# A sparse memory stage: every eighth gathered row is added on VectorE, with split scores, compact keys and a ninth ring place

## The reference

```python
q = (x @ Wq + bq).reshape(-1, 8, 128); q1, q2 = q[..., :64], q[..., 64:]
s1 = einsum('bhc,hnc->bhn', q1, keys[:, 0]); s2 = einsum('bhc,hnc->bhn', q2, keys[:, 1])   # 256 scores each
s1t, i1 = top_k(s1, 8); s2t, i2 = top_k(s2, 8)
scores, best = top_k(s1t[..., :, None] + s2t[..., None, :], 8)    # best 8 of 64 sums
indices = i1 * 256 + i2 at best
inner = einsum('bd,bhkd->bhk', x, w_down[indices])
vals = relu(inner) * softmax(scores)
out = einsum('bhk,bhkd->bd', vals, w_up[indices])
```

## Time and profile before

| what | value |
|---|---|
| median of 3 runs | 3177.79 us (3175.93 to 3196.16) |
| the profiled execution | 3188.18 us, span 3186.4 us |
| busy share of the span: TensorE, VectorE, ScalarE, GpSimd | 83%, 48%, 22%, 32% |
| start of the memory stage (end of the block before) | 2005.4 us |
| first row product of tile 0 | 2134.1 us |
| row products of the stage | 640, in ten tiles |

### The profile page before, as it was taken

How to read it: one execution, slowest core, us unless ns; L and a number is a source line. 1 busy time by engine, 2 the same in 40 slices (tenths; PEclk the granted TensorE clock), 3 DMA queues, 4 the chain that set the end, 5 groups by cost and what they waited for, 6 DMA issues and landing times.

```text
span 3186.4 us, 28032 instructions
## 1 busy us (share of the span) xinstructions
PE 2657.5 (83%) x8756; PEld 1463.4 (46%) x8756; DVE 1516.1 (48%) x3729; ACT 700.5 (22%) x1527; POOL 1010.8 (32%) x823
## 2 busy tenths in 40 slices
PE   2897887998770299999899888789898998998887
PEld 1564555665330044444366455554544544454322
DVE  3556448999200000000122545157657656666675
ACT  0233222121210000110033422123232323322322
POOL 0003343444344200000000000026566556656676
PEclk9898998999895599999999989899999999999999
DMA  9601306676210123023300040038898898889998
GB/s 209 204 0 21 89 1 190 200 216 187 43 7 1 32 78 79 0 62 112 92 1 0 0 148 0 7 110 314 284 329 312 297 314 308 309 311 332 344 366 349
DMA packets 237785, 498.58 MB, mean 156 GB/s; under 512 B 98553, under 2 KB 98928, under 8 KB 233546
## 3 DMA queue, kind: packets, MB, share of 16 engines
q0 software_dynamic: 158720, 336.03, 31.5%
q1 hardware_dynamic: 76425, 156.38, 16.5%
q10 hardware_dynamic: 2550, 5.12, 0.4%
HBM read 476.77 MB, written 20.34 MB: 156 GB/s over the span
## 4 chain that ended last, share of the span: by engine, by line
PE 49%; DMA 26%; DVE 11%; issue 7%; POOL 3%; ACT 2%; another core or an unknown queue 1%; SPq 1%; POOLq 0%; DVEq 0%; ACTq 0%
DMA adj<-e_cnt,e_idx 21%; PE bank L1018 10%; PE bank L1243 10%; PE bank L1233 3%; PE bank L1223 3%; PE bank L1003 2%; PE bank L581 2%; PE bank L1180 2%; PE bank L562 2%; PE bank L550 2%; PE bank L557 2%; PE bank L1192 2%; DVE qv L1471 2%; DMA qv<-in_L_ffn_rows,qv 2%; PE bank L770 1%
## 5 line engine op out<-in xcount | busy, mean ns | idle before, releaser
L283 POOL DMA_INDIRECT adj<-e_cnt,e_idx x160 | 344.2, 2151 | 740.4 <-DMA adj<-e_cnt,e_idx 446.8
L1243 PE MATMUL bank<-qv,stage 125*125 125x512 f32 x640 | 346.2, 633 | 65.6 <-DVE qv L1479 31.2
L1318 ACT ACTIVATE stage<-ident,qv 125x125 f32<-125x125 f32 x640 | 242.4, 397 | 481.7 <-DVE qv L1471 253.6
L1018 PE MATMUL bank<-big,wreg 125*125 125x512 f32 x400 | 173.4, 596 | 159.2 <-DMA wreg<-adj 159.2
L1471 DVE SCALAR_TENSOR_TENSOR qv<-qv 125x512 f32<-125x512 f32 x320 | 237.2, 745 | 143.8 <-DMA qv<-in_L_ffn_rows,biasb 74.4
L1143 POOL MEMSET wreg<- 64x2048 f32 x2 | 3.6, 1800 | 916.2 <-DVE h L700 916.1
L852 DVE SCALAR_TENSOR_TENSOR qv<-wreg,att_b,qv 128x2048 f32<-128x2048 f32 x120 | 276.9, 2349 | 6.9 <-DVE qv L852 0.2
L1149 POOL DMA_INDIRECT qv<-in_L_ffn_rows,qv x160 | 164.8, 1030 | 218.8 <-DVE qv L1413 113.9
L1243 PEld LDWEIGHTS bank<-qv,stage 125*125 125x125 f32 x640 | 113.8, 195 | 208.1 <-ACT stage L1318 91.2
L1149 POOL DMA_INDIRECT qv<-in_L_ffn_rows,biasb x160 | 163.9, 1025 | 112.7 <-PE bank L1243 90.7
L1018 PEld LDWEIGHTS bank<-big,wreg 125*125 125x125 f32 x400 | 75.6, 189 | 257.0 <-issue 257.0
(11 more groups left out here) (220 smaller groups left out, 4232.2 us busy)
## 6 DMA issues: line engine op xcount, KB each, us to landing
wreg<-in_L_gnn_basis SPq DMA_DIRECT2D x60, 1024.0 KB, 5.6
big<-in_L_mix_W SPq DMA_DIRECT2D x4, 4096.0 KB
adj<-wreg SPq DMA_DIRECT2D x5, 2187.5 KB
wreg<-adj SPq DMA_DIRECT2D x10, 1093.8 KB
qv<-adj SPq DMA_DIRECT2D x10, 1093.8 KB
big<-cells_t SPq DMA_DIRECT2D x1, 8750.0 KB
adj<-e_cnt,e_idx POOLq DMA_INDIRECT x160, 3.7
qv<-in_L_ffn_rows,qv POOLq DMA_INDIRECT x160, 5.9
```

What stands on the lines that cost most here:

```text
L283: nc.gpsimd.indirect_dma_start(out=adj, out_offset=bass.IndirectOffsetOnAxis(ap=e_idx[:, g:g + 1], axis=0), in_=e_cnt[:, g:g + 1], in_offs ...
L1018: mm = nc.tensor.matmul(psum[j][0:P, :], slabs[gl][:, j, c, :], zrel[:, c, :], start=(c == 0), stop=(c == COLT - 1))
L1243: nc.tensor.matmul(psum[7][0:P, :], diags[:, s % DRING, :], ring[s % RING][0:P, DIM:ROW], start=(s == 0), stop=(s == SLOTS - 1), skip_grou ...
L1318: nc.scalar.activation(diags[:, s % DRING, :], ident[0:P, 0:P], ACT.Relu, scale=inner[:, s:s + 1]).then_inc(p_diag, 1)
```

## The change

- Every eighth row of a tile (slots 7, 15, ... 63) gets no diagonal and no row product. After its dot VectorE clamps `inner` at zero and adds `inner` times the up half to a running sum `extra` in SBUF (for slot 7 it writes it). `take` adds `extra` to the node's value first, then bank 7. The place is freed by the new semaphore `p_add`.
- The keys are stored compactly (`keys_t`, 8 x 256 columns, both halves on 64 partitions each). A head's score is two matmuls of 64 partitions and 256 columns, into banks 3 and 4, and waits for the search of the head just before. The two memsets go, and four copies of 128 partitions replace eight of 64.
- The space that this frees holds a ninth ring place, used in turn over tile borders.
- TensorE issues a row product one slot later than its place in the order (`LAG`).
- The order moves: transposes at slot 0, queries at slots 1 to 5, scores at 8, 12, ... 36; the search in slots 9 to 39, three steps in four slots, the rest of it from 40 to 48; `take` after dot 1.

```diff
@@ -43,8 +43,7 @@
 SLOTS = PKH * TOPK
-RING = 8
-ROUNDS = SLOTS // RING
+RING = 9
 DRING = 8
...
@@ -155,13 +154,13 @@
-        keybd = wflat[:, 4096:8192].rearrange("p (h n) -> p h n", h=PKH)
+        keys_t = wflat[:, 4096:6144].rearrange("p (h n) -> p h n", h=PKH)
         wqf = wflat[:, 0:4096].rearrange("p (k n) -> p k n", k=KC)
...
         ROW = 2 * DIM
-        ring = [region[0:128, at + ROW * n:at + ROW * n + ROW] for region, at, count in ((qv, 5592, 4), (ctx_flat, 0, 1), (stage, 4048, 1), (big, 18384, 2))
+        ring = [region[0:128, at + ROW * n:at + ROW * n + ROW] for region, at, count in ((qv, 5592, 4), (ctx_flat, 0, 1), (stage, 4048, 1), (big, 18384, 2), (wflat, 6144, 1))
                 for n in range(count)]
...
@@ -1077,26 +1077,49 @@
+        extra = wflat[0:P, 7168:7168 + DIM]
+        BESIDE = 8
...
-        TURN_AT = 1
-        QUERY_AT = [2 + hh for hh in range(PKH)]
-        SCORE_AT = [10 + 3 * hh for hh in range(PKH)]
-        TAIL_AT = 35
-        EXP_AT = 42
+        LAG = 1
+        TURN_AT = 0
+        QUERY_AT = [1 + hh - hh // 2 for hh in range(PKH)]
+        SCORE_AT = [8 + 4 * hh for hh in range(PKH)]
+        SEARCH_AT = SCORE_AT[0] + 1
+        TAIL_AT = SEARCH_AT + 4 * PKH - 1
+        EXP_AT = TAIL_AT + 5
...
-        TAKE_AT = 3
+        TAKE_AT = 1
+        def aside(s):
+            return s % BESIDE == BESIDE - 1
+        def rows_of(pe, n):
+            return n - n // BESIDE if pe else n // BESIDE
+        def freed(engine, n):
+            if aside(n % SLOTS):
+                engine.wait_ge(p_add, rows_of(False, n + 1))
+            else:
+                engine.wait_ge(p_up, rows_of(True, n + 1))
...
-            return 16 * (t * ROUNDS + s // RING + 1)
+            return 16 * ((t * SLOTS + s) // RING + 1)
+        def place(t, s):
+            return (t * SLOTS + s) % RING
...
@@ -1139,16 +1162,14 @@
             pool.wait_ge(m["hat"], ADDS["hat"] + 2 + 2 * TILES)
-            for s in range(2):
-                nc.gpsimd.memset(keybd[64 * s:64 * s + 64, :, NKEYS * (1 - s):NKEYS * (2 - s)], 0.0).then_inc(p_keysS, 1)
             for t in range(TILES):
...
                     if t * SLOTS + s >= RING:
-                        pool.wait_ge(p_up, t * SLOTS + s - RING + 1)
+                        freed(pool, t * SLOTS + s - RING)
                     nc.gpsimd.indirect_dma_start(
-                        out=ring[s % RING], out_offset=None, in_=a["L0_ffn_rows"],
-                        in_offset=bass.IndirectOffsetOnAxis(ap=slots_of[t % 2][:, s:s + 1], axis=0)).then_inc(s_row[s % RING], 16)
+                        out=ring[place(t, s)], out_offset=None, in_=a["L0_ffn_rows"],
+                        in_offset=bass.IndirectOffsetOnAxis(ap=slots_of[t % 2][:, s:s + 1], axis=0)).then_inc(s_row[place(t, s)], 16)
...
@@ -1185,11 +1206,14 @@
                     pe.wait_ge(p_q, t * PKH + hh + 1)
-                    if hh >= 2:
-                        pe.wait_ge(p_top, t * TOPN + 4 * (hh - 1))
+                    if hh:
+                        pe.wait_ge(p_top, t * TOPN + 4 * hh)
                     elif t:
-                        pe.wait_ge(p_top, (t - 1) * TOPN + 4 * (PKH - 1 + hh))
-                    nc.tensor.matmul(psum[3 + hh % 2][0:P, :], pq_t[:, hh, :], keybd[:, hh, :], start=True, stop=True).then_inc(p_s_pe, 1)
+                        pe.wait_ge(p_top, (t - 1) * TOPN + 4 * PKH)
+                    for s in range(2):
+                        rows = slice(64 * s, 64 * s + 64)
+                        mm = nc.tensor.matmul(psum[3 + s][0:P, 0:NKEYS], pq_t[rows, hh, :], keys_t[rows, hh, :], start=True, stop=True)
+                    mm.then_inc(p_s_pe, 1)
                     yield
...
@@ -1239,9 +1263,15 @@
                     pe.wait_ge(p_out, t)
-                pe.wait_ge(p_diag, t * SLOTS + s + 1)
-                nc.tensor.matmul(psum[7][0:P, :], diags[:, s % DRING, :], ring[s % RING][0:P, DIM:ROW], start=(s == 0), stop=(s == SLOTS - 1),
+                if aside(s):
+                    return
+                pe.wait_ge(p_diag, rows_of(True, t * SLOTS + s + 1))
+                nc.tensor.matmul(psum[7][0:P, :], diags[:, s % DRING, :], ring[place(t, s)][0:P, DIM:ROW], start=(s == 0), stop=(s == SLOTS - 2),
                                  skip_group_check=True).then_inc(p_up, 1)
+            def late(n):
+                if n >= 0:
+                    row(n // SLOTS, n % SLOTS)
...
@@ -1258,24 +1288,23 @@
                 for s in range(SLOTS):
-                    for _ in range((s == TURN_AT) + (s in QUERY_AT) + (s in SCORE_AT)):
+                    for _ in range((s == TURN_AT) + QUERY_AT.count(s) + SCORE_AT.count(s)):
                         next(ahead, None)
...
                         next(beside, None)
-                    row(t, s)
+                    late(t * SLOTS + s - LAG)
                 for _ in ahead:
...
                     pass
+            for n in range(LAG):
+                late(TILES * SLOTS - LAG + n)
...
             act.wait_ge(p_w, 32)
-            for s in range(2):
-                for b in range(4):
-                    rows = slice(64 * s, 64 * s + 64)
-                    nc.scalar.activation(keybd[rows, 2 * b:2 * b + 2, NKEYS * s:NKEYS * s + NKEYS],
-                                         psum[2 + b][rows, :].rearrange("p (h m) -> p h m", h=2), ACT.Copy).then_inc(p_keysS, 1)
+            for b in range(4):
+                nc.scalar.activation(keys_t[:, 2 * b:2 * b + 2, :], psum[2 + b][:, :].rearrange("p (h m) -> p h m", h=2), ACT.Copy).then_inc(p_keysS, 1)
...
@@ -1312,9 +1341,11 @@
             def diag(t, s):
+                if aside(s):
+                    return
                 act.wait_ge(p_dot, t * SLOTS + s + 1)
                 if t * SLOTS + s >= DRING:
-                    act.wait_ge(p_up, t * SLOTS + s - DRING + 1)
+                    act.wait_ge(p_up, rows_of(True, t * SLOTS + s - DRING + 1))
                 nc.scalar.activation(diags[:, s % DRING, :], ident[0:P, 0:P], ACT.Relu, scale=inner[:, s:s + 1]).then_inc(p_diag, 1)
...
@@ -1357,12 +1388,12 @@
                 for s in range(2):
-                    nc.vector.max(top_v[:, hh, s, :], psum[3 + hh % 2][0:P, NKEYS * s:NKEYS * s + NKEYS]).then_inc(p_top, 1)
+                    nc.vector.max(top_v[:, hh, s, :], psum[3 + s][0:P, 0:NKEYS]).then_inc(p_top, 1)
                 n += 2
...
                     dve.wait_ge(p_top, n)
-                    nc.vector.max_index(top_i[:, hh, s, :], top_v[:, hh, s, :], psum[3 + hh % 2][0:P, NKEYS * s:NKEYS * s + NKEYS]).then_inc(p_top, 1)
+                    nc.vector.max_index(top_i[:, hh, s, :], top_v[:, hh, s, :], psum[3 + s][0:P, 0:NKEYS]).then_inc(p_top, 1)
                     yield
...
@@ -1465,17 +1496,33 @@
             def dot(t, s):
-                dve.wait_ge(s_row[s % RING], landed(t, s))
+                dve.wait_ge(s_row[place(t, s)], landed(t, s))
                 if s == 0:
                     dve.wait_ge(p_x, t + 1)
-                nc.vector.scalar_tensor_tensor(ring[s % RING][0:P, 0:DIM], ring[s % RING][0:P, 0:DIM],
+                nc.vector.scalar_tensor_tensor(ring[place(t, s)][0:P, 0:DIM], ring[place(t, s)][0:P, 0:DIM],
                                                probs_of[t % 2].rearrange("p h k -> p (h k)")[:, s:s + 1], xl[:, t % 2, :],
                                                ALU.mult, ALU.mult, accum_out=inner[:, s:s + 1]).then_inc(p_dot, 1)
+                if aside(s):
+                    k = rows_of(False, t * SLOTS + s)
+                    dve.wait_ge(p_dot, t * SLOTS + s + 1)
+                    nc.vector.tensor_scalar(inner[:, s:s + 1], inner[:, s:s + 1], 0.0, None, ALU.max).then_inc(p_rel, 1)
+                    dve.wait_ge(p_rel, k + 1)
+                    up = ring[place(t, s)][0:P, DIM:ROW]
+                    if s < BESIDE:
+                        if t:
+                            dve.wait_ge(p_ex, t)
+                        nc.vector.tensor_scalar(extra, up, inner[:, s:s + 1], None, ALU.mult).then_inc(p_add, 1)
+                    else:
+                        dve.wait_ge(p_add, k)
+                        nc.vector.scalar_tensor_tensor(extra, up, inner[:, s:s + 1], extra, ALU.mult, ALU.add).then_inc(p_add, 1)
...
                     dve.wait_ge(s_out[t % 2], 16 * (t // 2))
-                dve.wait_ge(p_up, (t + 1) * SLOTS)
+                dve.wait_ge(p_add, rows_of(False, (t + 1) * SLOTS))
+                nc.vector.tensor_tensor(h[:, t, :], h[:, t, :], extra, ALU.add).then_inc(p_ex, 1)
+                dve.wait_ge(p_up, rows_of(True, (t + 1) * SLOTS))
+                dve.wait_ge(p_ex, t + 1)
                 nc.vector.tensor_tensor(acc_of[t % 2], psum[7][0:P, :], h[:, t, :], ALU.add).then_inc(p_out, 1)
...
@@ -1501,7 +1548,7 @@
                         normed(half_of(t) // 2)
-                    if SCORE_AT[0] < s < TAIL_AT:
+                    if SEARCH_AT <= s < TAIL_AT and (s - SEARCH_AT) % 4 < 3:
                         next(ahead, None)
```

3 lines of the change are left out of this document (2 added, 1 removed).

## The result

The changed kernel takes **3155.77 us** (median of 7 runs, 3148.97 to 3165.97), the kernel before 3190.74 us in the runs beside it (7 runs, 3175.93 to 3198.40; the 3177.79 above was the median of the first three). The ratio taken from all runs is 0.9901, 95% interval 0.9873 to 0.9929: faster by 1.0%; the two medians are 35.0 us apart, 1.1%.

The account below looks back on a forecast made before the run. TensorE bounds tiles 0 to 6, issue and transfer the later ones. Gains of 45 (tiles 0 to 6), 10 (7 and 8) and 3 (9), less 8.5 in the front, make 49.5: 3177.8 to 3128 us; 8 in 10 range 3090 to 3165.

Parts of the forecast that it names:

- half given back: Rival in VectorE's stretches: aside 1.7 us, score 1.2, perhaps GpSimd issues 0.4 longer; 3155 us, chance 0.22.
- aside: Added VectorE work after each eighth dot, a clamp and a multiply-add: 1.0 us, 8 in a tile; bounds 0.7 and 1.7.
- T(0) to T(40): T(n) is the start of row n's product; in tiles 0 to 6 this stretch falls from about 71.8 to 65.0 us.
- T(40) to T(49): In tiles 0 to 6 VectorE bounds it: 16.6 us less 1.25 of lead, 15.4 instead of 13.6.
- T(49) to T(62): In tiles 0 to 6, the wait for row 62's place, landing, dot and product: 14.7 us instead of 16.7.
- even boundary: T(62) to next T(0): 11.3 us instead of 9.5 after an even tile, 4.7 instead of 7.0 after an odd one.
- the slower rival: Chain through the single score bank: an aside of 3.5 us costs some 10 us a tile; 3220 us, chance 0.10.
- side by side: Rival: a score's two halves run in parallel, 0.43 us instead of 0.86, 28 us more gain; 3100 us, chance 0.26.
- already counted: The lag of one slot hides only the 1.25 us from dot to product, which other terms already include.
- Front of tile 0: Before the first row product, single score bank spaces heads 2.8 us apart instead of 1.60: 8.5 us lost.
- Tiles 7 to 9: Last tiles, without feed-forward pieces: 10 us gained in tiles 7 and 8, 3 us in tile 9.
- just hidden: Tiles 7 and 8: four slots take 5.4 us by issue, VectorE's own work 4.3, or 5.3 with an aside.

Follow-up runs that it names:

- e1_no_aside: Changed kernel with all 64 rows of a tile through TensorE and nothing added on VectorE; 3150.41 us, ratio 0.9876 to the kernel before.
- g3_before_lag_all_order: Kernel before with the one-slot lag, the new boundary order and the later search; 3146.60 us, ratio 0.9886 to the kernel before.
- a0_after: The changed kernel measured again, unaltered, in a second series; 3152.41 us, ratio 0.9896 to the kernel before.
- f5_front_banks: Changed kernel with scores in the front of tile 0 going to two pairs of banks by turns; 3155.73 us, ratio 0.9872 to the kernel before.
- g2_before_lag_boundary: Kernel before with the one-slot lag and the new boundary order, old search slots; 3153.65 us, ratio 0.9912 to the kernel before.
- f6_front_banks_no_aside: Changed kernel with two pairs of score banks in the front of tile 0 and all 64 rows on TensorE; 3159.11 us, ratio 0.9899.
- f3_old_boundary: Changed kernel with transposes at slot 1, queries at slots 2 to 6, sum after dot 3, lag kept; 3185.74 us, ratio 0.9980.
- f4_lag0: Changed kernel with each row product in its own slot again, new boundary kept; 3186.17 us, ratio 0.9974 to the kernel before.

## Why the prediction was right or wrong

The direction and the range held: 3155.77 lies within 3090 to 3165. It is not within the forecast's own range (3112 to 3145) but at the time of "half given back", 3155. That is luck for this rival, whose terms did not come: an aside costs 0.98 us and not 1.7, a score 0.72 and not 1.2. The forecast of 3128 was 27.8 us low. Of these, 13.0 are the median of before, which rose from 3177.8 to 3190.7 as more runs came; the rest is gain that did not come: 49.5 forecast, 35.0 measured. Whether "faster by over 1%" came out can't be said: the medians give 1.1%, the ratio 0.99% with an interval that reaches to 0.9929, and the time that the prediction had named for it, below 3146, was not reached. The forecast also counts T(0) to T(40) from 71.8 us, which is the mean of tiles 1 to 6; with tile 0 it is 71.4, so that its sum for seven tiles holds some 3 us that were not there to be gained.

**Tiles 0 to 6: right as a sum.** 724.8 forecast (769.8 - 45), 729.4 and 723.8 measured. Step by step in tile 2: T(0) to T(40) 65.0 forecast, 65.8 measured; T(40) to T(49) 15.4, 14.8; T(49) to T(62) 14.7, 15.8 (15.0 to 15.3 in the mean); even boundary 11.3, 10.5; odd 4.7, 5.3.

**VectorE bounds T(40) to T(49): right.** The dots of slots 40 and 49 of tile 2 (against the earlier trace rows):

```profile
2396.28 0.73 DVE L1502 SCALAR_TENSOR_TENSOR big<-big,qv 125x512 f32<-125x512 f32 x1
...
2412.87 0.75 DVE L1502 SCALAR_TENSOR_TENSOR big<-big,qv 125x512 f32<-125x512 f32 x1
```

VectorE takes 16.59 us, forecast 16.6. Product 40 starts 3.04 after its dot and product 49 at 1.28, so TensorE eats 1.76 of lead, where I took 1.25.

**The aside at 1.0 us: right.** In tile 9, from the dot of an aside slot to the next dot:

```profile
3121.13 0.75 DVE L1502 SCALAR_TENSOR_TENSOR qv<-qv 125x512 f32<-125x512 f32 x1 [0.52 <-DMA qv<-in_L_ffn_rows,biasb]
...
3121.93 0.15 DVE L1508 TENSOR_SCALAR qv<-qv 125x1 f32<-125x1 f32 x1
3122.11 0.75 DVE L1517 SCALAR_TENSOR_TENSOR wreg<-qv,wreg 125x512 f32<-125x512 f32 x1
3122.78 0.75 DVE L1502 SCALAR_TENSOR_TENSOR qv<-qv 125x512 f32<-125x512 f32 x1
```

1.65 us in all, of which a dot is 0.67: the aside adds 0.98. With it the slower rival falls, whose point was 2.9.

**The two score products: assumed 0.86, measured about 0.72.** The chain of the changed kernel in tile 2 (start, us, what) has a score between row products:

```profile
2344.93 2.58 PE bank L1269 x6
2347.50 0.63 PE bank L1215 x4
2348.13 1.91 PE bank L1269 x4
```

The second half starts 0.01 us after the first, and the four records are done in 0.63; ahead of them some 0.09 more is lost than between row products. This fits both statements of the Trainium skill, "TensorEngine Tiling (Array Packing)", Key Properties: tiles of different rows do run side by side, and a change of tiling mode costs something. The price of side by side was not 0.43, as that rival had it, but it was nearer to it than to 1.2. The 0.14 a score, 8 us in seven tiles, did not show up as a gain of its own: T(0) to T(40) of tile 2 came out 0.8 above the forecast. Without asides TensorE is busy for 697.6 us in tiles 0 to 6 with split scores and nine places (`e1_no_aside`) and for 705.6 with whole scores and eight (`g3_before_lag_all_order`), so the 8 us of work are gone, but T(9) to T(40) is shorter by only 0.2 us a tile (53.7 against 53.9).

**The boundary.** The steps are right in size. The odd one, behind tile 3 (against the earlier trace rows):

```profile
2540.09 0.69 DVE L1523 TENSOR_TENSOR h<-h,wreg 125x512 f32<-125x512 f32 x1
...
2540.89 0.69 DVE L1526 TENSOR_TENSOR projbd<-bank,h 125x512 f32<-125x512 f32 x1
...
2541.63 2.07 PE L1269 MATMUL bank<-ctx_flat,stage 125*125 125x512 f32 x2
```

The new addition costs 0.80 in place of 0.6, and the last addition is again 0.74 ahead of the product. The even one, behind tile 2 (against the earlier trace rows):

```profile
2431.32 0.69 DVE L1482 BATCH_NORM_STATS2 st<-h 125x6 f32<-125x512 f32 x1
...
2436.17 0.55 DVE L1496 TENSOR_SCALAR qv<-h,small,rs 125x512 f32<-125x512 f32 x1
...
2436.77 1.09 PE L1193 MATMUL bank<-ident,qv 125*128 125x125 f32 x4 [4.92 <-issue]
```

The transposes take 1.09 us in this row, where I took 1.8 at 1.2 GHz; that is most of the 0.8 us by which the even boundary came out shorter.

**To which part the gain of tiles 0 to 6 belongs: right, with the lag left out.** The terms of the sum can be put against three steps that the runs show. The order (boundary, lag and search) has in the forecast 1.8 + 1.6 - 0.86 for T(0) to T(40) and the change of the two gaps without the added work of VectorE, some 23 us in seven tiles; measured 22.4 (769.8 to 747.4). The split scores and the ninth place have 0 and 2.0 a tile, 14 us; measured 10.6 (747.4 to 736.8), of which 8.1 lie in T(49) to T(62), and eight places instead of nine cost 8.1 too. The asides have 4.3 a tile, less 0.6 or 1.0 at the boundary and the 1.8 by which T(40) to T(49) was to grow, some 12 us; measured 13.0 (736.8 to 723.8). The 1.8 are put to them here because the runs do so: T(40) to T(49) is 13.7 with the later search alone and 14.8 with asides. That the medians show no gain of the last two steps has its reason outside of these tiles. From the order alone to the whole change the front grows by 12.2 us and tiles 7 and 8 by 3.3 (in `a0_after`, without the stops), and the stage as a whole falls only from 1150.4 to 1141.5 us. Such 9 us are within the intervals.

**What failed in it is the lag.** The prediction gave it nothing, "already counted". In the kernel before that is so (0.9986), but in the changed one taking it out costs 29.9 us in tiles 0 to 6. The boundary, on the other hand, is worth about the same in both: 21.0 us in tiles 0 to 6 of the kernel before, with the lag, and 16.3 of the changed one. Why the lag is worth so much beside the other parts was not tested. That it covers the disturbance which the asides and the shared score bank bring into VectorE's rhythm would explain it; the interplay is measured, this cause of it is argued only. Neither the changed kernel without asides nor one with two score banks was run without the lag.

**Front of tile 0: the mechanism right, the size too small.** 8.5 forecast, 13.6 measured. The term for a round was 2.8 us; it was 2.59 at full clock and 3.10 at half clock, as TensorE idles between scores. Two banks (`f5_front_banks`) give 9.5 us back. `g2_before_lag_boundary`, with two banks too, has a front of 130.9, 2.3 above before: the transposes and the first query, which now stand ahead of T(0). The rest fits the order too: in the changed kernel the old boundary has a front of 138.3 us, 4.0 shorter, and 9.5 + 4.0 = 13.5, if the two add up. For the work that now stands ahead of T(0) of tile 0 the forecast had no term.

**Tiles 7 to 9: wrong.** 13 us of gain were forecast; 7.0 came in `a0_after` (4.6 and 2.4) and -14.5 in the first profile. Two things are in this. The first is that T(40) to T(62) was to take 30.4 us and takes 32.5. The search in slots 40 to 48 makes T(40) to T(49) 3.5 us longer even in the kernel before (15.7 against 12.2), and the asides cost 4.8 us a tile in all (187.5 against 178.0 for two): T(40) to T(49) is 16.7 with them and 15.7 without, T(49) to T(62) 15.8 and 14.1, T(9) to T(40) 40.8 and 39.4. I had called the round of four slots with an aside "just hidden". The second is that in some executions all engines of the core stop for up to 5 us, several times in these tiles. VectorE near slot 43 of tile 8 of the changed kernel:

```profile
3022.41 0.23 DVE L1414 FIND_INDEX8 qv<-qv 125x8 uint32<-125x64 f32 x1
...
3024.91 0.23 DVE L1414 FIND_INDEX8 qv<-qv 125x8 uint32<-125x64 f32 x1 [0.61 <-issue]
3025.62 0.09 DVE L1414 MATCH_VALUE_LOAD qv<-qv 125x8 f32 x1 [0.48 <-issue]
3026.34 0.23 DVE L1414 FIND_INDEX8 qv<-qv 125x8 uint32<-125x64 f32 x1 [0.62 <-issue]
3028.55 0.20 DVE L1420 TENSOR_SCALAR qv<-qv 125x64 uint32<-125x64 uint32 x1 [1.98 <-remote]
```

Instructions that follow each other within 0.15 us elsewhere are 0.7 apart, with nothing shown that released them, while the DMA share is 1.03 at 410 GB/s. TensorE stands 4.38 us and falls to half clock. Such stops need no aside; in tile 7 of `f6_front_banks_no_aside` VectorE, ScalarE, TensorE and GpSimd all stand idle at 2894 us:

```profile
2894.68 0.76 DVE L1399 MAX8 qv<-bank 125x8 f32<-125x256 f32 x2 [3.65 <-remote]
```

Idle times of VectorE over 1.5 us that the profile gives to nothing on this core ("remote") are in five of the fourteen profiles, from tile 7 on: this one and the four whose labels begin with f. In two of these, T(40) to T(49) has them in both tiles (20.8 and 21.5 here, 20.8 and 21.9 in `f3_old_boundary`), in `f4_lag0` (20.4) and `f5_front_banks` (19.9) in one. There are none in the other nine. Tiles 7 to 9 take 297.0 us here and 275.5 in `a0_after`, so they cost some 21 us. Full DMA engines are not enough for one: in `a0_after` the share is 1.02 (384 GB/s) over 6.2 us at the same distance behind T(40) of tile 8, without a stop. The cause stays open.

**GpSimd, part of the rival of half given back.** The claim was that each new multiply-add lengthens an issue by 0.4. Single issues take from 0.93 to 1.44, as they did before the change (up to 1.46):

```profile
2988.63 1.44 POOL L1170 DMA_INDIRECT big<-in_L_ffn_rows,qv  x1 [0.30 <-issue]
2990.37 0.93 POOL L1170 DMA_INDIRECT wreg<-in_L_ffn_rows,qv  x1 [0.30 <-issue]
```

The mean over tiles 7 and 8 hardly moved: 131.80 / 127 = 1.04 in `a0_after`, 127.89 / 126 = 1.02 without asides. That is 0.02 x 64 = 1.5 us a tile at most, not 3.3; issues over 1.2 us are 21 of 127 with asides and 14 of 126 without. The rule on the shared port (the Trainium skill, "SBUF — State Buffer", SBUF: two separate sides) is not contradicted by the mixed issue times, but no run shows that it is their cause, and the price is a small part of the 4.8 us.

## What to carry to other kernels

Before work is moved between engines, look at where the bounding engine waits at the seams between tiles: here reordering a few slots around one sum and one set of transposes came within the noise of the whole change. Work taken off the bounding engine pays only in the stretches where it bounds, and is paid for in those where its new engine does; price both, in every kind of tile. Here the terms for the tiles with most work were right, and what they won was given back in the front and in the last tiles. Not all edits to an order add up: test each alone and each left out, since the lag was worth nothing in one kernel and 30 us in the other. The versions to keep are `g3_before_lag_all_order` or, without the later search, `g2_before_lag_boundary`, which the runs don't tell apart: within the intervals they are as fast as the changed kernel, and they leave out the asides, the split scores and the ninth place.

## What was not expected of the hardware

- Two float32 products on different 64 partitions, into different banks, start 0.01 us apart and take 0.63 together, where a 512-column product takes 0.86; about 0.09 more goes at the change of shape.
- A chain between two engines can halve the clock of one: with 1.88 us of idleness in each round of 3.10 the granted clock of the stretch was 0.63, and the same score went from 0.70 to 1.22 us.
- An execution of the same kernel can lose some 21 us in three tiles to stops of all engines at once (297.0 against 275.5 us), and the untouched part ahead of the stage ends between 1985.4 and 2018.6 us. A single profile can mislead about a change of 1%.
